# A three-layer transformer block on one core: another hand-written timetable for the work beside the FFN tiles, routing in 26 steps, four hidden buffers

## The reference, cut to what matters

```python
x = x + 0.5 * ffn(layernorm(x))
x = x + mixer(layernorm(x))
x = x + 0.5 * ffn(layernorm(x))

def ffn(t):                                       # 32 experts of 64 hidden units, 4 chosen per token
    scores = sigmoid(t @ router_w.T); s = scores + router_bias
    group_score = sum of the two best s in each of 4 groups of 8 experts; keep 2 groups
    chosen = top 4 of s in the kept groups
    w = 2.5 * scores[chosen] / sum(scores[chosen])
    return sum_e w_e * down_e(silu(gate_e(t)) * up_e(t)) + shared_expert(t)

def mixer(t):
    gate, val = t @ W_in.T
    v = depthwise_conv5(val) + conv_b
    y = scan(h = tanh(a) * h + sigmoid(gate) * v)
    return layernorm(t + y @ W_out.T) * ln_w + ln_b
```

## Time and profile before

| | |
|---|---|
| median of 3 runs | 722.85 us (722.22 to 723.27) |
| the profiled execution | 722.28 us |
| its span, first to last instruction | 720.5 us |
| mean granted PE clock | 0.992 of full speed |
| 8 transfers per unit of weights to all partitions | 256 to 640 KB each, median 4.1, 7.6 and 13.3 us to landing |

### The profile page before, as it was taken

The page is one execution under the profiler, slowest core; times in us unless marked ns, Lnnn a source line. Parts: engine busy times, 40 slices in busy tenths (PEclk is TensorE's granted clock), DMA queues, the critical chain, the costliest instruction groups (busy, mean ns, idle before and its releaser), DMA issues. The chain is left out here.

```text
span 720.5 us, 10391 instructions
## 1 busy us (share of the span) xinstructions
PE 667.3 (93%) x3016; PEld 523.0 (73%) x3016; DVE 582.6 (81%) x1547; ACT 419.5 (58%) x801; POOL 477.4 (66%) x709
## 2 busy tenths in 40 slices
PE   5579999998989999989999899999999899999997
PEld 5457786777766777867877677776777678777785
DVE  4778697788978878887797978989698887978765
ACT  4436665664655566566656565655665565665553
POOL 1147767865677767777667775777676866687673
PEclk9899999999999999999999999999999999999999
DMA  8492907408464290833909075370916428090370
GB/s 194 96 208 56 216 1 160 93 1 180 88 147 91 51 213 19 182 71 85 182 23 212 18 163 105 83 155 20 221 28 145 108 66 173 13 216 24 86 167 16
DMA packets 60010, 78.84 MB, mean 109 GB/s; under 512 B 7696, under 2 KB 27184, under 8 KB 59952
## 3 DMA queue, kind: packets, MB, share of 16 engines
...
## 5 line engine op out<-in xcount | busy, mean ns | idle before, releaser
L487 POOL TENSOR_TENSOR hid_lo<-hid,hid_hi 128x256 fp32r<-128x256 f32 x540 | 389.9, 746 | 199.9 <-ACT hid_hi L584 199.0
L584 ACT ACTIVATE hid_hi<-hid 128x512 fp32r<-128x512 f32 x272 | 170.6, 627 | 125.1 <-DVE hid L735 123.1
L722 DVE TENSOR_TENSOR weighted<-gate_ps,raw 128x512 f32<-128x512 f32 x256 | 175.1, 684 | 67.1 <-ACT gate_ps L576 54.3
L576 ACT ACTIVATE gate_ps<-gate_ps 128x512 f32<-128x512 f32 x256 | 148.5, 580 | 97.8 <-PE gate_ps L1010 94.5
L735 DVE TENSOR_TENSOR hid<-weighted,up_ps 128x512 f32<-128x512 f32 x256 | 174.7, 682 | 13.8 <-DVE weighted L722 0.5
L1053 PE MATMUL down_ps<-hid_hi,wt_hi 128*128 128x512 f32 x272 | 108.6, 399 | 5.8 <-ACT ffn_sb L588 5.7
L1056 PE MATMUL down_ps<-hid_lo,wt_hi 128*128 128x512 f32 x272 | 107.9, 397 | 0.2 <-DVE hid_lo L743 0.2
L1054 PE MATMUL down_ps<-hid_hi,wt_lo 128*128 128x512 f32 x272 | 107.7, 396 | 0.0
L1008 PE MATMUL up_ps<-xT_hi,wt_hi 128*128 128x512 f32 x187 | 77.9, 417 | 12.2 <-DVE hid L735 11.9
L1008 PE MATMUL gate_ps<-xT_hi,wt_hi 128*128 128x512 f32 x187 | 80.3, 430 | 5.7 <-DVE weighted L722 5.6
L1010 PE MATMUL up_ps<-xT_hi,wt_lo 128*128 128x512 f32 x187 | 74.4, 398 | 0.0
...
## 6 DMA issues: line engine op xcount, KB each, us to landing
raw<-wT_hbm SPq DMA_DIRECT2D x64, 640.0 KB, 13.3
...
```

Source lines behind the costliest of these rows:

```text
L487: last = nc.gpsimd.tensor_tensor(hid_lo[s][:, cols], hid[s][:, cols], hid_hi[s][:, cols].bitcast(F32), ALU.subtract)
L576: nc.scalar.activation(bank[:, :] if j else silu_sb[:, :], bank[:, :], ACT.Silu).then_inc(silu_done, 1)
L584: nc.scalar.activation(hid_hi[s][:, :], hid[s][:, :], ACT.Copy).then_inc(hid_hi_done, 1)
L722: V.tensor_tensor(weighted[j % 2][:, :], gate_ps[n % BANKS][:, :], wb[:, j - 1, :], ALU.mult)\
```

## The change

- `RING` goes from 3 to 4.
- Routing is issued by `route_step(k, b, st, n)`, one of 26 steps, each with its own slot; `even(first, last)` spreads them evenly over the half slots. `logits` is no step of its own any more.
- Five 16-column temporaries of routing move from SBUF to free columns of the PSUM bank `routed`.
- The chain of the mixer is split in steady units: norm, transposes and the two projections stay beside (4,m) (`PROJECT`); convolution, scan, output product and sum move beside the next (1,m) (`MIXER`). The norm work behind it (`NORM4`) moves from the (1,m) unit to the (4,m) unit after it.
- The side products on PE move to about two slots behind what they need (router two slots behind the transposes instead of one, transposes of a norm at slot 0 of the unit behind it, the transposes of an FFN output two or three slots behind the copy).
- The first down product of a unit moves from slot 3 to slot 4, where two down products stand together.
- The tanh of the mixer gate gets one more wait, for the scan of the block before.

```diff
-RING = 3
+RING = 4
...
-        n_best = sb("n_best", [P, TT * NG])
-        far_single = sb("far_single", [P, TT * NG])
+        n_best = routed[:, 388:388 + TT * NG]
+        far_single = routed[:, 404:404 + TT * NG]
         best1_tied = sb("best1_tied", [P, TT * NG])
-        best_other = sb("best_other", [P, TT * NG])
-        best2 = sb("best2", [P, TT * NG])
+        best_other = routed[:, 420:420 + TT * NG]
+        best2 = routed[:, 436:436 + TT * NG]
...
-        grank = sb("grank", [P, TT * NG])
+        grank = routed[:, 452:452 + TT * NG]
...
+        def even(first, last, n=ROUTE):
+            return tuple(first + int(i * (last - first) * 2 / (n - 1) + 0.5) / 2 for i in range(n))
...
-        FIRST = {..., "router 1": 3, "logits 1": 3.5, "silu logits 1": 4,
-                 "route 1": (4.5, 5, 5.5, 6, 6.5, 7, 7.5, 8, 9, 9.5, 10), "weights 1": 12}
-        NEXT = {"stats 1": 11.5, "meanvar 1": 12, "norm 1": 13, "normalise 1": 14}
-        PREPARE = {"transpose 1": 1, "xT high 1": 1, "xT low 1": 1.5, "router 1": 2, "logits 1": 2.5,
-                   "silu logits 1": 3, "route 1": (4, 4.5, 5.5, 6, 6.5, 7, 8, 8.5, 9, 9.5, 10), "weights 1": 12}
-        CHAIN = {"copy ffn 1": 2, "transpose ffn 1": 3, "add ffn 1": 3.5, "stats 2": 4, "meanvar 2": 4,
-                 "norm 2": 4, "normalise 2": 5, "add ln_b": 9, "transpose 2": 7, "xT high 2": 7,
-                 "xT low 2": 7.5, "mixer gate": 9, "tanh gate": 9, "mixer value": 10, "copy value": 10,
-                 "conv": (11, 11.5, 12, 12.5, 13, 13.5), "y high": 14, "y low": 14,
+        FIRST = {..., "router 1": 4, "silu logits 1": 5, "route 1": even(4, 12), "weights 1": 13}
+        NEXT = {"stats 1": 12.5, "meanvar 1": 13, "norm 1": 14, "normalise 1": 15}
+        PREPARE = {"transpose 1": 0, "xT high 1": 0, "xT low 1": 0.5, "router 1": 2, "silu logits 1": 3,
+                   "route 1": even(2, 12), "weights 1": 13}
+        PROJECT = {"copy ffn 1": 2, "transpose ffn 1": 4, "add ffn 1": 4, "stats 2": 5, "meanvar 2": 6,
+                   "norm 2": 6, "normalise 2": 7, "transpose 2": 9, "xT high 2": 9, "xT low 2": 9,
+                   "mixer gate": 11, "tanh gate": 11, "mixer value": 12, "copy value": 12, "add ln_b": 15}
+        MIXER = {"conv": (0, 0.5, 1, 2, 3, 4), "y high": 5, "y low": 5, "mixer out": 8, "mixer sum": 8,
+                 "stats 3": 14}
+        NORM4 = {"meanvar 3": 0, "norm 3": 0, "normalise 3": 1, "scale 3": 2, "x2": 12, "stats 4": 12.5,
+                 "meanvar 4": 13, "norm 4": 14, "normalise 4": 15}
+        XT4 = {"transpose 4": 0, "xT high 4": 0, "xT low 4": 0.5}
+        ROUTE4 = {"router 4": 2, "silu logits 4": 3, "route 4": even(2, 12), "weights 4": 13}
+        OUTPUT = {"copy ffn 4": 2, "transpose ffn 4": 5, "halve ffn": 5, "add ffn 4": 8}
...
+        WHOLE = {**PROJECT, "add ln_b": 9, "conv": (12, 12.5, 13, 13.5, 14, 14.5), "y high": 15, "y low": 15,
                  "mixer out": 16, "mixer sum": 16.5}
-        NORM4 = {"stats 3": 0, "meanvar 3": 0.5, "norm 3": 1, "normalise 3": 2, "scale 3": 3, "x2": 4.5, "stats 4": 5,
-                 "meanvar 4": 5, "norm 4": 6, "normalise 4": 7, "transpose 4": 14, "xT high 4": 14, "xT low 4": 14.5}
-        ROUTE4 = {"router 4": 1, "logits 4": 1.5, "silu logits 4": 2,
-                  "route 4": (2.5, 3.5, 5.5, 6, 6.5, 7, 8, 8.5, 9, 9.5, 10.5), "weights 4": 12}
-        OUTPUT = {"copy ffn 4": 2, "transpose ffn 4": 3, "halve ffn": 3, "add ffn 4": 6}
...
             if (k, b) == (1, 1):
-                return at(CHAIN, 0) + at(PREPARE2, 2)
+                return at(WHOLE, 0) + at(PREPARE2, 2)
             if (k, b) == (1, 2):
-                return at(NORM4_0, 0) + at(ROUTE4_0, 0) + at(CHAIN1, 1) + at(NEXT, 3)
+                return at(NORM4_0, 0) + at(ROUTE4_0, 0) + at(PROJECT1, 1) + at(NEXT, 3)
             if (k, b) == (4, 0):
-                return at(REST1, 1) + at(NORM4_1, 1) + at({**CHAIN, "add ln_b": 16}, 2) + at(PREPARE, 3)
-            if (k, b) == (1, 3):
-                return at(XT4_1, 1) + at(ROUTE4_1, 1) + at(NORM4, 2) + at(OUTPUT, 0) + at(NEXT, 4)
+                return at(MIXER1, 1) + at(NORM4_1, 1) + at(PROJECT2, 2) + at(PREPARE, 3)
+            if (k, b) == (1, NBLK - 1):
+                return (at(MIXER6, b - 1) + at(NORM4_6, b - 1) + at(XT4, b - 2) + at(ROUTE4, b - 2)
+                        + at(OUTPUT, b - 3))
             if (k, b) == (4, NBLK - 3):
-                return at(CHAIN, NBLK - 1) + at(ROUTE4, NBLK - 2)
+                return at(XT4, b + 1) + at(ROUTE4, b + 1) + at(WHOLE, b + 2)
...
             if k == 1:
-                return (at(NORM4, b - 1) + at(ROUTE4, b - 2) + at(OUTPUT, b - 3)
-                        + (at(NEXT, b + 1) if b < NBLK - 1 else []))
-            return at(CHAIN, b + 2) + at(PREPARE, b + 3)
+                return (at(MIXER, b - 1) + at(XT4, b - 2) + at(ROUTE4, b - 2) + at(OUTPUT, b - 3)
+                        + at(NEXT, b + 1))
+            return at(NORM4, b + 1) + at(PROJECT, b + 2) + at(PREPARE, b + 3)
...
+            def route_step(k, b, st, n):
+                if n == 0:
+                    dve.wait_ge(logits_ready[k], b + 1)
+                    return st.done(V.tensor_scalar(tiny[:, :, :], side_te, -1e-9, 1e-8, ALU.is_ge, ALU.mult))
+                if n == 3:
+                    dve.wait_ge(logit_silu_done[k], b + 1)
+                st.wait()
...
-            for part in range(PARTS):
-                for n in range(4 + 2 * part, min(6 + 2 * part, NBATCH)):
-                    weight_low(n)
-                route_part(1, 0, first, part)
+            for step in range(3, ROUTE):
+                if step % 2 and 4 + step // 2 - 1 < NBATCH:
+                    weight_low(4 + step // 2 - 1)
+                route_step(1, 0, first, step)
...
-                    if j >= LAG:
+                    if j == LAG + 1:
+                        down(k, m, 0)
+                    if j > LAG:
                         down(k, m, j - LAG)
```

More of the change, by code:

```diff
@@ L299, in macaron_kernel @@
-        ROUTE4 = {"router 4": 1, "logits 4": 1.5, "silu logits 4": 2,
-                  "route 4": (2.5, 3.5, 5.5, 6, 6.5, 7, 8, 8.5, 9, 9.5, 10.5), "weights 4": 12}
-        OUTPUT = {"copy ffn 4": 2, "transpose ffn 4": 3, "halve ffn": 3, "add ffn 4": 6}
-        PREPARE2 = {"stats 1": 0.5, "meanvar 1": 0.5, "norm 1": 1, "normalise 1": 2, "transpose 1": 4, "xT high 1": 4,
-                    "xT low 1": 4.5, "router 1": 5, "logits 1": 5.5, "silu logits 1": 6,
-                    "route 1": (6.5, 7, 7.5, 8, 8.5, 9, 9.5, 10, 10.5, 11, 11.5), "weights 1": 13}
@@ L307, in macaron_kernel @@
-        NORM4_0 = {**NORM4, "transpose 4": 8, "xT high 4": 8, "xT low 4": 8.5, "scale 3": 2, "x2": 3, "stats 4": 3.5,
-                   "meanvar 4": 3.5, "norm 4": 4, "normalise 4": 5}
-        ROUTE4_0 = {"router 4": 9, "logits 4": 9.5, "silu logits 4": 10,
-                    "route 4": (10.5, 11, 11.5, 12, 12.5, 13, 13.5, 14, 14.5, 15, 15.5), "weights 4": 16}
-        CHAIN1 = {**CHAIN, "transpose 2": 10, "xT high 2": 10, "xT low 2": 10.5, "mixer gate": 12, "tanh gate": 12,
-                  "mixer value": 13, "copy value": 13, "conv": (16, 16, 16.5, 16.5, 16.5, 16.5)}
@@ L314, in macaron_kernel @@
-        REST1 = {}
-        for step in ("y high", "y low", "mixer out", "mixer sum"):
-            del CHAIN1[step]
-        REST1 = {"y high": 1, "y low": 1, "mixer out": 4, "mixer sum": 4.5, "stats 3": 10.5}
+        def even(first, last, n=ROUTE):
+            return tuple(first + int(i * (last - first) * 2 / (n - 1) + 0.5) / 2 for i in range(n))
+        FIRST = {"norm 1": 0, "normalise 1": 0, "transpose 1": 2, "xT high 1": 2, "xT low 1": 2.5, "router 1": 4,
+                 "silu logits 1": 5, "route 1": even(4, 12), "weights 1": 13}
@@ new lines, in macaron_kernel @@
+        PREPARE2 = {"stats 1": 0, "meanvar 1": 0.5, "norm 1": 1, "normalise 1": 1, "transpose 1": 3, "xT high 1": 3,
+                    "xT low 1": 3.5, "router 1": 5, "silu logits 1": 6, "route 1": even(5, 12), "weights 1": 13}
+        WHOLE = {**PROJECT, "add ln_b": 9, "conv": (12, 12.5, 13, 13.5, 14, 14.5), "y high": 15, "y low": 15,
+                 "mixer out": 16, "mixer sum": 16.5}
+        NORM4_0 = {"stats 3": 0, "meanvar 3": 0.5, "norm 3": 1, "normalise 3": 2, "scale 3": 2, "x2": 3, "stats 4": 3.5,
+                   "meanvar 4": 3.5, "norm 4": 4, "normalise 4": 5, "transpose 4": 7, "xT high 4": 7, "xT low 4": 7}
@@ L318, in macaron_kernel @@
+        ROUTE4_0 = {"router 4": 9, "silu logits 4": 10, "route 4": even(9, 15.5), "weights 4": 16}
+        PROJECT1 = {**PROJECT, "transpose 2": 10, "xT high 2": 10, "xT low 2": 10.5, "mixer gate": 12,
+                    "tanh gate": 12, "mixer value": 13, "copy value": 13}
+        MIXER1 = {**MIXER, "stats 3": 10.5}
         NORM4_1 = {"meanvar 3": 10.5, "norm 3": 11, "normalise 3": 12, "scale 3": 13, "x2": 14.5,
                    "stats 4": 15, "meanvar 4": 15, "norm 4": 16, "normalise 4": 16}
```

(12 more changed lines are left out.)

119 lines of the change are left out of this document (48 added, 71 removed).

## The result

The changed kernel took 729.6 us (median of 6 runs, 725.5 to 735.0) against 722.2 us (720.6 to 723.3) of the kernel before beside it: ratio 1.011, interval 1.006 to 1.016. It is slower by 1.1%, where 703 was forecast. The profiled execution took 730.95 us with a span of 729.2; its mean granted clock was 0.977, before it was 0.992. The six runs spread more than those of before, and with the clock: 725.5 us at 0.986, 735.0 at 0.972.

The account below looks back on a forecast made before the run. PE, busy 93% of the span, was taken as the floor, with only its stalls (59 us behind the setup) to win; terms summed to 20.0 us off the 720.5 us span, giving 700.5 and a median of 703, range 690 to 716.

Parts of the forecast that it names:

- The steady pairs: Units (4,m) with (1,m): stall 3.3 us per pair instead of 6.25; 10.0 us gained over three pairs and (4,4).
- How it enters slot 0: Norm in slot 14, normalise in 15: silu of tile 16 about 2 us late, priced at 0.6 us stall per unit.
- the slower rival: Transposes at slot 0 wait in every unit from (1,1) to (4,6), margin only 0.65 us: 730 us, chance 0.09.
- Edges: Units where the schedule starts and ends, such as (1,1), (1,2), (4,5), (4,6): gains of 0.5 to 3.3 us each term.
- (d): (1,3) and (4,5), slot 0: transposes one slot behind `normalise 4`; forecast PE wait about 3.2 us and cost 2.0.
- (c): (1,1) and (4,5), slot 16: mixer output one slot behind its scan's parts; forecast 1.2 and 1.0 us lost.
- (a): (1,1), slots 1 to 3: `normalise 1` in the slot of `norm 1`, ACT stops for POOL; no wait forecast.
- (b): (1,2), slots 7 to 9: transposes, high and low part of `4` in one slot behind `normalise 2`; no wait forecast.
- (e): (4,6), slot 5: halving queued on ACT behind a normalisation, transposes of `4` need its bank; no wait forecast.
- Less what DVE regains: Edge unit (1,1): mixer product 1.5 us later, reduced by DVE's relief to 1.2 us lost, 0.5 net gain.
- Five temporaries in PSUM: Routing: tiny operations fall to 0.18 us, saving 1.1 us of DVE per routing; `beats` expected to stay at 0.23.
- First down product: Moved to slot 4: takes away 1.7 us each in (1,1) and (1,2), 0.8 in (4,6), 0.4 to 0.6 in steady units.

Follow-up runs that it names:

- heat run: The changed kernel with PE multiplying zeros at six of its stops at the edges, so that it does not stand still: 722.6 us.
- five: The changed kernel with the steps at all five stopping places at the edges, (a) to (e), set apart: 714.5 us.
- five_ps: Kernel five with the routing temporary `gdiff` in PSUM too, so that `beats` has only one SBUF input: 713.9 us.
- five_sb: Kernel five with the five 16-column routing temporaries back in SBUF: 717.8 us.
- five_lag: Kernel five with the first down product of a unit back in slot 3: 715.3 us.
- five_ring: Kernel five with three buffers of the hidden tile again instead of four: 714.0 us.

## Why the prediction was wrong

**The steady pairs: right.** 10.0 forecast, 11.2 measured, 9.9 without the product that only moved; pair 81.8 forecast, 81.4 measured. The terms inside it were the wrong way round. With some 39.2 of PE's work in each unit I had 2.2 of stall for (1,m) and 1.1 for (4,m), with waits for `hid` in slots 4 to 6 of (1,m). Measured were 39.65 us for (1,m), next to no stall, and 41.7 to 42.1 for (4,m). So slots 0 to 4 of (1,m), the densest by my walk, cost nothing; which of the walk's terms was too high was not tested.

**How it enters slot 0, and the slower rival: the margin held.** No transposes wait in steady units. The rival gave 730 and the kernel took 729.6, but its mechanism, a wait in every unit, did not occur: agreement of the number is no agreement of the cause.

**Edges: the step that failed.** I had 0.5 for (1,1), 3.3 for (1,2), 0.5 for (1,7) and (4,5), 1.2 for (4,6): 5.5 together, and measured were -21.4. That is 26.9 of the 28.7 us between the forecast of the span (20.0 less) and what came (8.7 more), 1.3 of it the moved product, for which the sum had no term. With the five places apart the kernel is at 714.5, and with two more waits gone at 706.9, still 3.9 over the forecast. Three things went wrong in it.
- I walked the edges only for the two pairs of steps that I had noticed, (d) and the late mixer product (c). Their waits were sized well: (d) at 3.2 in (1,3) and 2.0 in (4,5), measured 3.6 and 1.9, and (c) at 1.5 less what is regained, 1.2 in (1,1) and 1.0 in (4,5), measured 1.8 in both. I credited the other gains without walking the slots of `PREPARE2`, `NORM4_0` and `OUTPUT` in (4,6), where (a), (b) and (e) lie. The diff of the tables shows them: a consumer moved into its producer's slot, or behind a slow step on the same engine, against what the change does elsewhere. The price was there as well: the earlier trace rows shows ACT waiting 1.85 us for POOL with a normalisation one slot behind its norm, and with both in the same slot it waited 3.23.
- The new stops had no price for PE's clock. I saw 0.96 in (1,3) in the earlier trace rows with 1.8 us of loss, and let only that stand. The heat run puts the item at 7.0 us.
- "Less what DVE regains" was credited at edges too, though at (a) and (d) PE waits for ACT behind POOL. That relief of DVE did not shorten these waits is read from the traces; no run took it apart.

**Five temporaries in PSUM: half right.** By the medians `best_tied` and `best2` fell to 168 and 170 ns and `gmask` from 357 to 164, as taken. But I let decide on `beats`, and it rose from 225 to 463 ns and `gdiff` from 218 to 426. The rule of the Trainium skill that I set aside (GPSIMD Engine Reference, section Specifications) was right: an operation with two SBUF inputs meets GpSimd. In five, `beats` took 207 to 1098 ns; with `gdiff` in PSUM (five_ps) it never took more than 225. About 0.45 of the 1.1 us per routing came back in `gdiff` and `beats` by the medians. By the means, which a few slow ones raise, it is 0.56 of 1.15. With the five back in SBUF (five_sb) `beats` is at 216 again by the median, but 364 by the mean, and `best_tied` and `best2` are at 372 and 168, far from their 600 and 658 of before. So part of what looked like the price of SBUF was the place in the schedule, and the five in PSUM are worth 0.5 us of DVE per routing there (8.2 us over 16). How the delay passes from one operation to another was not tested. By the pair of five_sb the whole thing moved 0.24 us, so this was not what mattered.

**First down product, four buffers, weights a slot later, tanh's wait:** no cost and no gain of their own, as said for the last three. In (1,1) and (1,2) I had counted 1.7 each for the down product; the copy's wait did go (0.3 left in the kernel), but the new stops took its place, and five_lag shows no time for it.

**Open**: why (4,0) stays at 47 to 51 us in every kernel here, and why the same schedule has its clock fall in (1,2) or (4,5) in one execution and not in another (five_ring ran (1,2) in 45.9 us, five in 49.0). (1,0), which no experiment on the changed kernel edits, took 39.1 to 43.8 us in their profiled executions, at clocks of 0.96 to 0.87. So lengths of single units, read from one execution each, are good to some 3 us where the clock falls; the medians of the kernels carry the argument, and the steady units, which agree to 0.2 us where their tables are the same.
